# Moving the scaling of the second layer's attention weights to ScalarE and the addition of beta's diagonal behind the turn

## What is computed

```python
def _L1_gnn_ref(x, W, a, beta, mask):
    h = jnp.einsum('bnc,cf->bnf', x, W)
    a1, a2 = (a[:F_, 0], a[F_:, 0])
    s1 = jnp.einsum('bnf,f->bn', h, a1)
    s2 = jnp.einsum('bnf,f->bn', h, a2)
    e = jax.nn.leaky_relu(s1[:, :, None] + s2[:, None, :], negative_slope=ALPHA)
    e = e * mask[None, :, :]
    att = jax.nn.softmax(e, axis=2)
    h_prime = jnp.einsum('bij,bjf->bif', att, h)
    return jax.nn.elu(h_prime + beta * h)

h = jnp.maximum(_layernorm(x, axis=-1), 0.0)
x = x + _L1_gnn_ref(h, L1_gnn_W, L1_gnn_a, L1_gnn_beta, adj)
```

## Time and profile before

| | us |
|---|---|
| median of 3 runs | 774.73 |
| lowest and highest of the 3 | 774.39, 776.27 |
| the profiled execution | 775.35 |
| its span, first to last instruction | 773.6 |
| busy: TensorE, its weight loads | 720.5, 667.8 |
| busy: VectorE, ScalarE, POOL | 646.1, 552.5, 486.3 |
| granted TensorE clock, mean (1.00 is 2.4 GHz) | 0.982 |

### The profile page before, as it was taken

How to read it: one execution, slowest core, us unless ns; L and a number is a source line. 1 busy time by engine, 2 the same in 40 slices (tenths; PEclk the granted TensorE clock), 3 DMA queues, 4 the chain that set the end, 5 groups by cost and what they waited for, 6 DMA issues and landing times.

```text
span 773.6 us, 23203 instructions
## 1 busy us (share of the span) xinstructions
PE 720.5 (93%) x7001; PEld 667.8 (86%) x7001; DVE 646.1 (84%) x2709; ACT 552.5 (71%) x1768; POOL 486.3 (63%) x615
## 2 busy tenths in 40 slices
PE   3999999999799999969999899999999999999995
PEld 3899999999577777759999799999999999999994
DVE  4688888887699999978998888888888888888873
ACT  2445455454377787855774699999999999999995
POOL 1254555545577778757886676666676666676653
PEclk9899999999899999988999999999999999999999
DMA  6223300000000000000000000000000000000001
GB/s 200 89 90 95 91 18 0 0 0 0 2 0 2 1 1 2 2 0 1 0 0 0 3 25 18 28 28 28 28 27 14 28 28 28 28 27 14 28 28 42
DMA packets 21662, 20.10 MB, mean 26 GB/s; under 512 B 2416, under 2 KB 21616, under 8 KB 21616
## 3 DMA queue, kind: packets, MB, share of 16 engines
q1 hardware_dynamic: 19440, 18.16, 7.5%
q10 hardware_dynamic: 2176, 1.44, 0.6%
HBM read 11.21 MB, written 8.39 MB: 25 GB/s over the span
## 4 chain that ended last, share of the span: by engine, by line
PE 75%; DVE 17%; issue 3%; POOL 1%; ACT 1%; DVEq 0%; POOLq 0%; ACTq 0%
PE bank L374 41%; PE bank L1058 7%; PE bank L1050 5%; PE bank L1068 4%; PE bank L152 4%; PE bank L426 4%; PE bank L439 3%; PE bank L354 3%; DVE stats L115 3%; DVE xs L829 2%; DVE masked_e L805 2%; DVE leaky_e L810 2%; DVE small L813 2%; PE bank L364 1%; DVE att L823 1%
## 5 line engine op out<-in xcount | busy, mean ns | idle before, releaser
L1127 ACT ACTIVATE prob<-wide,small 128x128 f32<-128x128 f32 x512 | 199.0, 395 | 20.1 <-DVE small L1211 20.1
L1176 POOL TENSOR_TENSOR prob<-prob,small 128x512 f32<-128x512 f32 x128 | 133.3, 1041 | 104.7 <-DVE small L1225 104.7
L141 POOL TENSOR_TENSOR rstd<-vare,mhalf 128x2 f32<-128x2 f32 x128 | 88.8, 693 | 74.2 <-DVE vare L130 74.2
L1211 DVE CUSTOM_DVE_ANT_0 wide<-bank,mbias 128x128 f32<-128x128 f32 x512 | 116.0, 283 | 9.4 <-PE bank L1050 9.4
L115 DVE BATCH_NORM_STATS2 stats<-xs 128x6 f32<-128x256 f32 (+1 forms) x256 | 95.4, 415 | 5.6 <-DMA xs<-in_x_dram 4.5
L1127 ACT ACTIVATION_READ_ACCUMULATOR prob<-wide,small 128x1 f32 x512 | 98.3, 192 | 0.0
L345 POOL TENSOR_SCALAR xn<-xs,nmean,rstd 128x256 f32<-128x256 f32 x126 | 69.0, 557 | 13.7 <-POOL rstd L141 10.8
L1134 ACT COPY probT<-bank 128x512 f32<-128x512 f32 x128 | 72.0, 588 | 6.4 <-PE bank L1058 5.4
L1058 PE MATMUL bank<-ident,prob 128*128 128x128 f32 x512 | 73.8, 276 | 1.9 <-POOL prob L1176 1.9
L364 PE MATMUL bank<-w,hT 128*128 128x258 f32 x256 | 63.2, 390 | 2.2 <-DVE xs L599 1.9
L1058 PEld LDWEIGHTS bank<-ident,prob 128*128 128x128 f32 x512 | 57.0, 140 | 8.9 <-issue 6.0
(11 more groups left out here) (131 smaller groups left out, 1838.7 us busy)
## 6 DMA issues: line engine op xcount, KB each, us to landing
out_dram<-xs SPq DMA_DIRECT2D x32, 256.0 KB, 2.2
xs<-in_x_dram SPq DMA_DIRECT2D x28, 256.0 KB, 2.7
xs<-in_x_dram ACTq DMA_DIRECT2D x1, 768.0 KB, 7.5
xs<-in_x_dram ACTq DMA_DIRECT2D x1, 256.0 KB, 3.7
wq<-in_L_gnn_Wq_dram SPq DMA_DIRECT2D x1, 256.0 KB, 3.4
wk<-in_L_gnn_Wk_dram SPq DMA_DIRECT2D x1, 256.0 KB, 5.7
wv<-in_L_gnn_Wv_dram SPq DMA_DIRECT2D x1, 256.0 KB, 7.5
w<-in_L_gnn_W_dram SPq DMA_DIRECT2D x1, 256.0 KB, 8.2
```

Of the source, the lines that this page charges most:

```text
L141: nc.gpsimd.tensor_tensor(rstd[:, b, :], vare[:, b, :], mhalf[:, :], ALU.pow).then_inc(rstd_ready, 1)
L1127: ins = nc.scalar.activation(prob[:, r, i, :], wide[:, r, i, :], ACT.Exp, bias=nmax[r][:, i:i + 1], scale=-1.0, accum_out=rsum[r][:, i:i + 1])
L1176: nc.gpsimd.tensor_tensor(prob[:, r, :, :], prob[:, r, :, :], rinv[r].unsqueeze(2).to_broadcast([128, QUAD, N]), ALU.mult).then_inc(prob_r ...
L1211: nc.vector.tensor_tensor_reduce(out=wide[:, r, i, :], in0=SS[r][:, i * N:(i + 1) * N], in1=mbias[:, :], scale=-1.0, scalar=3e38, op0=ALU. ...
```

## The change

The scaling by the inverse sums leaves VectorE: normalise(p) on ScalarE, at the end of its step, writes att from exp_e with the inverse sums as scale, without beta. copy_pT(p) leaves ScalarE: add_beta(p) on VectorE takes the turned weights out of PSUM and adds beta_ident, the diagonal, in the same operation, into attT. In VectorE's step it stands as add_beta(p-2) behind inverse(p-1), where attention(p-1) stood; elu(p-4) follows. TensorE's and POOL's lists are the same. prob_ready is now given by ScalarE, pt_ready by VectorE. The tails are reordered to match.

```diff
--- before.py
+++ after.py
@@ -714,11 +714,6 @@
                     act.wait_ge(att_done, since(p - 3))
                     nc.scalar.copy(valb[p % 4][:, :, :], HG[:, :, 0:D + 2]).then_inc(val_ready, 1)
 
-                def copy_pT(p):
-                    act.wait_ge(pt_done, p + 1)
-                    act.wait_ge(att_done, since(p))
-                    nc.scalar.copy(attT[:, :, :], PT[:, 0:2 * N].rearrange("p (g n) -> p g n", g=2)).then_inc(pt_ready, 1)
-
                 def copy_hT(p):
                     act.wait_ge(tr_done, p + 1)
                     nc.scalar.activation(hT_flat, HT[:, :], ACT.Relu).then_inc(hT_ready, 1)
@@ -730,6 +725,13 @@
                         ins = nc.scalar.activation(exp_e[:, g, :], leaky_e[:, g, :], ACT.Exp, bias=nmax[:, g:g + 1],
                                                    accum_out=rsum[:, g:g + 1])
                     ins.then_inc(exp_ready, 1)
+
+                def normalise(p):
+                    act.wait_ge(rinv_ready, p + 1)
+                    act.wait_ge(pt_done, since(p))
+                    for g in range(2):
+                        ins = nc.scalar.activation(att[:, g, :], exp_e[:, g, :], ACT.Copy, scale=rinv[:, g:g + 1])
+                    ins.then_inc(prob_ready, 1)
 
                 def elu_negative(p):
                     act.wait_ge(att_done, p + 1)
@@ -744,8 +746,6 @@
 
                 def step(p):
                     copy_h(p)
-                    if p >= 2:
-                        copy_pT(p - 2)
                     if p + 1 < PAIRS:
                         copy_hT(p + 1)
                     if p >= PAIRS - 2:
@@ -758,18 +758,19 @@
                         softmax_exp(p - 1)
                     if p >= 3:
                         elu_exp(p - 3)
+                    if p >= 1:
+                        normalise(p - 1)
 
                 for p in range(PAIRS):
                     step(p)
-                copy_pT(PAIRS - 2)
                 softmax_exp(PAIRS - 1)
                 act.wait_ge(l2_yt_done, 1)
                 nc.scalar.copy(yT_high[0], HT[:, :]).then_inc(l2_high_ready, 1)
+                normalise(PAIRS - 1)
                 elu_negative(PAIRS - 3)
                 elu_exp(PAIRS - 3)
                 act.wait_ge(l2_yt_done, 2)
                 nc.scalar.copy(yT_high[1], bank[1][:, :]).then_inc(l2_high_ready, 1)
-                copy_pT(PAIRS - 1)
                 relu_norm(act, 2, 0, xn, l2_shift_ready).then_inc(l2_xn_ready, 1)
                 elu_negative(PAIRS - 2)
                 elu_exp(PAIRS - 2)
@@ -816,13 +817,11 @@
                     dve.wait_ge(exp_ready, p + 1)
                     nc.vector.reciprocal(rinv, rsum).then_inc(rinv_ready, 1)
 
-                def attention(p):
-                    dve.wait_ge(rinv_ready, p + 1)
-                    dve.wait_ge(pt_done, since(p))
-                    for g in range(2):
-                        ins = nc.vector.scalar_tensor_tensor(att[:, g, :], exp_e[:, g, :], rinv[:, g:g + 1], beta_ident[:, :],
-                                                             ALU.mult, ALU.add)
-                    ins.then_inc(prob_ready, 1)
+                def add_beta(p):
+                    dve.wait_ge(pt_done, p + 1)
+                    dve.wait_ge(att_done, since(p))
+                    nc.vector.tensor_tensor(attT[:, :, :], PT[:, 0:2 * N].rearrange("p (g n) -> p g n", g=2),
+                                            beta_ident[:, :].unsqueeze(1).to_broadcast([128, 2, N]), ALU.add).then_inc(pt_ready, 1)
 
                 def elu(p):
                     dve.wait_ge(added, p + 1)
@@ -843,7 +842,8 @@
                     root_argument(dve, ahead, step_sem, ready_sem, (p + 1) % 2)
                     if p >= 1:
                         inverse(p - 1)
-                        attention(p - 1)
+                    if p >= 2:
+                        add_beta(p - 2)
                     if p >= 4:
                         elu(p - 4)
 
@@ -853,12 +853,13 @@
                 inverse(PAIRS - 1)
                 dve.wait_ge(l2_high_ready, 1)
                 nc.vector.tensor_tensor(yT_low[0], HT[:, :], yT_high[0].bitcast(F32), ALU.subtract).then_inc(l2_yt_ready, 1)
-                attention(PAIRS - 1)
+                add_beta(PAIRS - 2)
                 elu(PAIRS - 4)
                 dve.wait_ge(l2_high_ready, 2)
                 nc.vector.tensor_tensor(yT_low[1], bank[1][:, :], yT_high[1].bitcast(F32), ALU.subtract).then_inc(l2_yt_ready, 1)
                 dve.wait_ge(l2_xn_ready, 2)
                 layer_norm_stats(dve, 3, l2_step, l2_stats_ready, 1)
+                add_beta(PAIRS - 1)
                 elu(PAIRS - 3)
                 elu(PAIRS - 2)
                 elu(PAIRS - 1)
```

## The result

| | before | changed |
|---|---|---|
| median, us | 775.02 (4 runs) | 854.83 (4 runs) |
| lowest to highest | 774.39 to 776.27 | 854.07 to 856.52 |
| the profiled execution | 775.35 | 854.18 |
| its span | 773.6 | 852.4 |
| ratio, 95% interval | | 1.1028 (1.1007 to 1.1049) |

The changed kernel is 79.8 us slower. 877 was forecast, with 836 to 904 as its range.

What follows compares the result with a forecast made beforehand. VectorE was taken to set 4.04 us a pair before, a ring of waits 6.28 after; with the clock low half the time, 7.60 a ring, +102.3 us on 775.4 gave 877.7, 877 against the median, range 836 to 904.

Steps and rivals of the forecast that it cites:

- the ring: Second layer: add_beta, attend, next product, turn, copy_hT, elu_negative, softmax_exp, inverse, next add_beta wait in a circle, one pair per turn.
- the prediction's VectorE list: VectorE's own work per pair: 0.20 us shorter than 4.04 us, so 3.84 us, but not counting.
- The ring's length: Sum of the steps and handovers from one add_beta to the next: 6.28 us a pair in place of 4.04.
- The clock: TensorE's wait of about 2.2 us in every pair makes its clock fall again and again and come back; partly low 0.60.
- The share: Part of the second layer's time at the lower clock, taken as half: mean ring 7.60 us, 877.7 us in all.
- The prediction's low ring: A pair with TensorE at the lower clock, attend, product and turned matrices slower: 9.61 us in place of 6.28.
- the signs named: Expected traces: 6.3 us pairs, waits before reciprocal, attend and copy_hT, product groups of 1.9 and 3.8 us, clock between 0.5 and 1.0.
- ScalarE nearer to PSUM: Skill's rule that ScalarE is closer to PSUM, VectorE to SBUF, speaking against the swap: 0.03 us a pair, 1 us in all.
- the first ring: The ring first acts on product(3), whose end moves from 213.45 to 215.56 us: +2.11.
- the tail: Behind product(31) to the last attend, 14.57 us before: same work in another sequence, nothing put, between -2 and +2.
- Clock holds: Rival: the ring closes and TensorE's clock stays high, 840 us (836 to 844); chance 0.22.
- No ring: Rival: VectorE's list stays the bound and its 0.20 us a pair are gained, 6 us, 769 us; chance 0.03.

Runs made afterwards that it cites:

- the two filler runs: Changed kernel with three, or one, more f32 products of 256 columns on TensorE between spread and attend: 831.95 us with three, 831.47 us with one.
- the ring closed in the kernel before: Kernel before with copy_pT(p-2) on ScalarE moved from behind copy_h(p) to behind softmax_exp(p-1), none of the change's work moved: 852.88 us.
- one link less: Changed kernel with elu_negative(p-3) on ScalarE moved from ahead of softmax_exp(p-1) to behind it: 819.13 us.

## Why the prediction was right, and where it was off

**What bounds the kernel, and the ring.** Right. VectorE's 4.04 us a pair gave way to the ring named in the prediction, link by link, and the saved VectorE time counted for nothing until the ring was cut: then a pair took 3.79 us, near the 3.84 of the prediction's VectorE list. ScalarE's two scalings took 0.69 us (0.6 to 0.8 was said), and hid.

**The ring's length.** 6.28 was summed, 6.00 measured. The mis-sized terms: reciprocal and addition, 0.67 with their handovers, took 0.03 + 0.08 + 0.42 = 0.53, because the addition doesn't wait for the reciprocal and overlaps it by 0.09; elu_negative to softmax_exp took 0.48, not 0.57; and turn ended 0.66 behind the product, not 0.70. From attend's load (267.05) to the end of the product (269.92) it was 2.87, as taken from before. In 28 rings the 0.28 makes 7.8 us.

**The clock.** This is the larger part of the 22 us between 877 and 855. The kind was right: it fell again and again behind the wait and came back, and the two filler runs, in which it didn't fall, took 23 us less. The share was a guess between two ends, half of the time, and it was a quarter: with 0.88 granted over the rings, (1 - 0.88) / 0.5 = 24% of the time. The price of low time was off the other way. The prediction's low ring loses 9.61 - 6.28 = 3.33 us in 9.61, about a third, since it spreads the low level over the whole ring, waits included. The low stretches lay on attend and the product, where TensorE was busy throughout: a fall cost 7.68 - 6.00 = 1.68 us and lasted some 3.4, half of it lost, and it came in every second ring. The two errors pull opposite ways, and that is luck. With 24% in place of half, the prediction's sum gives 856; with the measured ring as well (6.00, and 9.33 when low) it gives 848, 7 too low. Counted by falls the sum closes: 28 x 6.00 + 14 x 1.68 + 0.97 - 113.57 + 2.11 = +81.0, 856.

In the rows of before, a low stretch lasted 6.5 us or more. In mid-layer of the changed kernel they were about half as long; attend and the product follow at once there and keep TensorE busy, but no run tries whether that is why. Two of the signs named did not come. No product group took 3.8 us: the clock was back before the product ended, and the slow ones took 2.66 to 2.79 us. And ScalarE's idle time stood before copy_h, 2.40 us for the product, not before copy_hT, which starts right behind turn's end (270.62, 270.58).

**The ends.** +1.75 for the first ring, against 2.11, and -0.8 in the tail, against 0 with 2 to either side; the relu of 0.97 in the last ring showed as 7.73 us there in place of a due 6.75.

**The rivals.** "Clock holds", 840, was the nearer to the truth with 15 us, and the forecast with 22; the truth lay between them, in the range. "No ring", 769, was named with the one point on which it decides, the exponential ahead of copy_h; built that way, the kernel took 766.4, of which the shorter list gave 6.1 us, the 6 of that rival, and the order of ScalarE's step, mostly at the layer's ends, the rest.

**ScalarE nearer to PSUM.** The rule of the Trainium skill, ScalarE: Activation LUTs, section Step-by-step: what each stage is for, stood beside the sum as 1 us. In the changed kernel VectorE's addition out of PSUM took 0.42 us and ScalarE's copy had taken 0.38, which over 28 pairs is as small as said. But this sets an addition against a copy, and the prediction's own pair, 0.38 and 0.41 us, sets a copy against a conversion to another type (L492 is a CAST); no run here tries the rule with one and the same operation.

The section HAM oscillation of the Trainium skill's page TensorE: Matmul & The Clock Gate described a loop of the kind that came. In its example the clock falls in every turn, behind waits of some 3 to 5 us. Here it fell in every second turn behind waits of 2.02 us, and was low for a quarter of the time.

## What to carry to other kernels

Moving a step to an engine with idle time is judged by its place in that engine's list, not by its duration: write down what stands ahead of it, what those wait for, and whether one of them waits for what the step itself releases. If a ring closes, its length is the time of a pair, and cutting one link (here one exponential moved up) can turn 10% slower into 1% faster. A repeated wait of TensorE can have a second price, the clock (23 us of the 80 here); a filler product in it is a quick way to measure the two apart.

## What the runs showed of the hardware

- The granted clock fell behind a repeated wait of 2.02 us (the changed kernel, every second pair) and of 1.74 us (the ring closed in the kernel before, about two of three pairs), and didn't fall in mid-layer with waits of 1.53 us (one link less) or of 1.58 and 1.30 us (one product of 0.60 us more in the pair). Which quality of the wait decides isn't settled by these runs.
- A low stretch of the clock lasted some 3.4 us in mid-layer of the changed kernel and cost 1.68 us with TensorE busy throughout; at the layer's last pairs in the kernel before one lasted 6.5 us or more.
- ScalarE's activation with a scale for each partition, 128x128 in SBUF, took 0.69 us for the two of a pair, from the first's start to the second's end, and the timeline shows no table load between it and the exponentials (the changed kernel).
- The addition of 128x256 starts 0.08 us behind a reciprocal of 2 columns that it doesn't depend on (272.57 and 272.49 in the changed kernel).
